# A grouped-convolution and mixed-experts chain: conv1 and the middle layer rebuilt from 32-row strips on row tiles, with the input rounded phase by phase

## The reference

```python
x = x + conv(x, W0)  + (cond @ cw0.T)[:, :, None] + bias      # 9 taps, 4 groups of 32 channels
x = x + (sum_k att1[b,k] * E1[k]) @ x + (att1 @ bias_k1)      # 8 experts, 128x128, 1x1 convolution
x = x + (sum_k att2[b,k] * E2[k]) @ x + (att2 @ bias_k2)
x = x + conv(x, W3)  + (cond @ cw3.T)[:, :, None] + bias      # as the first
```

## Time and profile before

| what | value |
|---|---|
| median of the runs | 2600.42 us |
| the profiled execution | 2600.42 us |
| its span, first to last instruction | 2598.5 us |
| TensorE busy | 2554.9 us, 98% |
| VectorE busy | 2277.4 us, 88% |
| ScalarE busy | 2077.8 us, 80% |
| queue with nearly all DMAs, share of 16 engines | 83.5% |
| mean granted TensorE clock | 0.995 of full |

### The profile page before, as it was taken

The page is one execution under the profiler, slowest core; times in us unless marked ns, Lnnn a source line. Parts: engine busy times, 40 slices in busy tenths (PEclk is TensorE's granted clock), DMA queues, the critical chain, the costliest instruction groups (busy, mean ns, idle before and its releaser), DMA issues.

```text
span 2598.5 us, 38320 instructions
## 1 busy us (share of the span) xinstructions
PE 2554.9 (98%) x11082; PEld 2071.6 (80%) x11082; DVE 2277.4 (88%) x3384; ACT 2077.8 (80%) x1940; POOL 3.7 (0%) x17
## 2 busy tenths in 40 slices
PE   6999999999999999999999999999999999999997
PEld 4788888888888888888888888888888888888885
DVE  7988888888888888888888888888888888888884
ACT  4788878888887888888788888878888887888885
POOL 0000000000000000000000000000000000000000
PEclk8999999999999999999999999999999999999998
DMA  5788888888888888888888888888888888888875
GB/s 193 284 317 317 320 318 314 321 324 316 317 320 318 313 321 324 316 316 320 318 314 321 324 316 316 321 318 313 321 323 317 317 320 317 315 320 322 317 300 210
DMA packets 335448, 808.75 MB, mean 311 GB/s; under 512 B 37066, under 2 KB 40146, under 8 KB 302674
## 3 DMA queue, kind: packets, MB, share of 16 engines
q1 hardware_dynamic: 333200, 807.16, 83.5%
q10 hardware_dynamic: 2242, 1.53, 0.2%
HBM read 137.45 MB, written 134.22 MB: 105 GB/s over the span
## 4 chain that ended last, share of the span: by engine, by line
PE 97%; DVE 2%; issue 0%; DMA 0%; ACT 0%; ACTq 0%; SPq 0%; DVEq 0%
PE pair L766 82%; PE quad L810 14%; PE pair L800 1%; DVE mixed L595 0%; PE quad L747 0%; DMA x_in<-in_x 0%; DVE w_hi L528 0%; DVE weighted L583 0%; DVE x_lo L504 0%; DVE x_lo L630 0%; DVE x_hi L627 0%; DMA x_ph<-x_ch 0%; DVE x_ch L569 0%; DVE w_lo L534 0%; DMA x_ch<-x_ph 0%
## 5 line engine op out<-in xcount | busy, mean ns | idle before, releaser
L766 PE MATMUL pair<-x_hi,w_hi 128*128 128x512 f32 x3072 | 1227.1, 399 | 8.7 <-DVE x_lo L643 5.4
L766 PE MATMUL pair<-x_hi,w_lo 128*128 128x512 f32 x3072 | 1213.1, 395 | 0.0
L766 PE MATMUL pair<-x_lo,w_hi 128*128 128x512 f32 x3072 | 1209.0, 394 | 0.0
L766 PEld LDWEIGHTS pair<-x_hi,w_lo 128*128 128x128 f32 x3072 | 579.6, 189 | 137.3
L766 PEld LDWEIGHTS pair<-x_hi,w_hi 128*128 128x128 f32 x3072 | 579.0, 188 | 136.4 <-DVE x_lo L643 5.8
L766 PEld LDWEIGHTS pair<-x_lo,w_hi 128*128 128x128 f32 x3072 | 581.6, 189 | 131.5
L595 DVE TENSOR_REDUCE mixed<-weighted 128x128 f32<-128x1152 f32 x256 | 576.9, 2254 | 0.1
L402 ACT COPY x_out<-x_ch 128x1024 f32<-128x1024 f32 x256 | 530.3, 2073 | 2.9 <-DMA x_ch<-x_ph 2.9
L351 ACT COPY x_ch<-x_in 128x1024 f32<-128x1024 f32 x256 | 531.0, 2076 | 1.9 <-DMA x_in<-in_x 1.9
L410 ACT COPY x_ph<-pair 128x512 f32<-128x512 f32 x512 | 314.8, 615 | 272.1 <-PE pair L766 272.1
L418 ACT ACTIVATE x_ph<-pair,bias_now 128x512 f32<-128x512 f32 x512 | 358.6, 700 | 216.2 <-PE pair L766 216.2
(11 more groups left out here) (80 smaller groups left out, 607.2 us busy)
## 6 DMA issues: line engine op xcount, KB each, us to landing
x_ph<-x_ch SPq DMA_DIRECT2D x1024, 256.0 KB, 2.6
x_ch<-x_ph SPq DMA_DIRECT2D x1024, 256.0 KB, 2.6
x_in<-in_x SPq DMA_DIRECT2D x128, 1024.0 KB, 5.5
out<-x_out SPq DMA_DIRECT2D x128, 1024.0 KB, 4.2
x_out<-in_W SPq DMA_DIRECT2D x8, 144.0 KB, 5.4
...
```

The source lines that it names most:

```text
L766: mm = nc.tensor.matmul(conv_bank[g % 2], w[l][:, m, g, :], x[:, g, m:m + N], start=(m == 0 and x is hi and w is w_hi), stop=(m == BLK - 1 ...
```

## The change

The program is rebuilt around one idea. Conv1 is computed in the **channel layout**: TensorE's 128 rows are used as four independent tiles of 32 rows, one for each group of 32 channels. For each of 12 strips (STRIPS = PH * BLK; strip d reads input phase d mod 4, shifted by d div 4) and each of the three parts, four matmuls of 32 rows by 512 columns are issued in a row, one per group, each into its own PSUM bank, each with its own 32x128 weights (`conv1_strips`). That is 144 matmuls where there were 36. Its output is in the phase layout, and the middle layer takes it as it is: 4 groups x 3 parts x 4 phases = 48 matmuls of 32 rows (`middle`), whose weights are rows of M laid out four times, once per phase (`m_rows`). Conv4 stays as it was, 36 matmuls of 128 rows. Two PSUM tiles of four banks, `banks[0]` and `banks[1]`, serve all layers: in step b conv1(b) and middle(b) use one, M(b+1) and conv4(b-1) the other.

What goes: the `cut` of x and the 4 DMAs of x to phase rows; the copy of x1 out of PSUM, its 4 DMAs back and its split from SBUF; the bias in the evacuation of x4. What comes:

- ScalarE rounds x straight from `x_in`, 2048 elements in one instruction that reads every fourth float (16 bytes apart) (`high_x`); VectorE's `low_x` reads `x_in` in the same way.
- ScalarE rounds x1 from PSUM in two halves (`high_x1`), VectorE subtracts from PSUM (`low_x1`).
- The bias of conv4 is added in `join`, which therefore waits for `bias4_ready`; VectorE's `set_bias4(b-2)` stands in its step b behind `split_x3(b-1)`.
- VectorE mixes the experts in 16 `scalar_tensor_tensor` instructions of 128x128 per batch in place of two products and two sums, and no longer carries the identity as a ninth expert.
- M is written to DRAM with one DMA (`save_m`) and read back with four (`spread_m`), from the same SyncE queue, a batch ahead.
- The order of ScalarE, VectorE, TensorE and SyncE is written anew.

The core of the diff, with lines of before marked - and of the changed kernel marked +:

```diff
-x_ch = sb("x_ch", [C, PH, N])
-x_ph = sb("x_ph", [C, G, N])
-x1_ph = sb("x1_ph", [C, G, N])
-x1_ch = sb("x1_ch", [C, PH, N])
+x_hi = sb("x_hi", [C, PH, N + 2 * HALO], f32r)
+w0_hi = sb("w0_hi", [C, STRIPS, PH, GROUP], f32r)
+m_saved = nc.dram_tensor("m_saved", [ODD, C, 2, C], f32).ap()
+m_rows = sb("m_rows", [C, ODD, G, 2, C], f32r)
+banks = [ctx.enter_context(nc.psum_tensor(f"banks{n}", [C, PH, N], f32)) for n in range(2)]
...
+    def save_m(b, slot):
+        sp.wait_ge(m_split, b + 1)
+        sp.dma_start(m_saved[slot, :, :, :], m_pair[:, :, :].bitcast(f32)).then_inc(m_stored, DMA)
+    def spread_m(b, slot):
+        sp.wait_ge(m_stored, DMA * (b + 1))
+        for q in range(PH):
+            sp.dma_start(m_rows[rows_of(q), slot, :, :, :].bitcast(f32),
+                         m_saved[slot, :, :, :].rearrange("(g c) t o -> c g t o", g=G)
+                         ).then_inc(m_spread, DMA)
...
+    def step(b, slot, first=False, load_next=True, last=False):
+        if not (first and slot == 0):
+            move_x3(b - 1)
+        if load_next:
+            load(b + 2, slot)
+        if not first:
+            store(b - 2, slot)
+        if not last:
+            save_m(b + 1, 1 - slot)
+        if not (first and slot == 0):
+            move_x4(b - 1, 0)
+        if not last:
+            spread_m(b + 1, 1 - slot)
+        if not (first and slot == 0):
+            move_x4(b - 1, 1)
...
-    def cut(b, slot, turn, half):
-        if half == 0:
-            act.wait_ge(x_loaded[slot], DMA * (turn + 1))
-            wait(act, x_moved, DMA * G * b)
-        phases = slice(half * PH // 2, (half + 1) * PH // 2)
-        nc.scalar.copy(x_ch[:, phases, :],
-                       x_in[:, slot, :].rearrange("c (n p) -> c p n", p=PH)[:, phases, :]
-                       ).then_inc(x_cut, 1)
-    def round_x(b):
-        act.wait_ge(x_moved, DMA * G * (b + 1))
-        wait(act, conv1_done, G * b)
-        nc.scalar.copy(x_hi[:, :, HALO:N + HALO], x_ph[:, :, :]).then_inc(x_hi_ready, 1)
+    def high_x(b, slot, turn):
+        act.wait_ge(x_loaded[slot], DMA * (turn + 1))
+        wait(act, conv1_done, G * b)
+        nc.scalar.copy(x_hi[:, :, HALO:N + HALO],
+                       x_in[:, slot, :].rearrange("c (n q) -> c q n", q=PH)
+                       ).then_inc(x_hi_ready, 1)
+    def high_x1(b, tile, half):
+        if half == 0:
+            wait(act, mid_done, PH * b)
+        act.wait_ge(conv1_done, G * b + (half + 1) * G // 2)
+        nc.scalar.copy(halves(x1_hi, half), halves(tile, half)).then_inc(x1_high, 1)
+    def join(b, slot, turn, half):
+        if half == 0:
+            act.wait_ge(x4_moved, DMA * G * (b + 1))
+            wait(act, x_stored[slot], DMA * turn)
+            act.wait_ge(bias4_ready, b + 1)
+        nc.scalar.activation(halves(x_out[:, slot, :].rearrange("c (n p) -> c p n", p=PH), half),
+                             halves(x4_ch, half), ACT.Identity, bias=bias4_now[:, :]
+                             ).then_inc(x_joined, 1)
+    def evacuate_x4(b, tile, half):
+        if half == 0:
+            wait(act, x4_moved, DMA * G * b)
+        act.wait_ge(conv4_done, G * b + (half + 1) * G // 2)
+        nc.scalar.copy(halves(x4_ph, half), halves(tile, half)).then_inc(x4_ready, 1)
+    def evacuate_x3(b, tile):
+        act.wait_ge(bias3_ready, b + 1)
+        act.wait_ge(mid_done, PH * (b + 1))
+        for half in range(2):
+            nc.scalar.activation(halves(x3_ch, half), halves(tile, half), ACT.Identity,
+                                 bias=bias3_now[:, :]).then_inc(x3_ready, 1)
+    def step(b, slot, turn, first=False, last=False):
+        if not first:
+            for half in range(2):
+                join(b - 2, slot, turn - 1, half)
+        for half in range(2):
+            high_x1(b, banks[slot], half)
+        if not last:
+            high_x(b + 1, 1 - slot, turn + slot)
+        if not (first and slot == 0):
+            for half in range(2):
+                evacuate_x4(b - 1, banks[1 - slot], half)
+        evacuate_x3(b, banks[slot])
...
+    def low_x(b, slot):
+        dve.wait_ge(x_hi_ready, b + 1)
+        nc.vector.tensor_tensor(x_lo[:, :, HALO:N + HALO],
+                                x_in[:, slot, :].rearrange("c (n q) -> c q n", q=PH),
+                                x_hi[:, :, HALO:N + HALO].bitcast(f32), ALU.subtract
+                                ).then_inc(x_lo_ready, 1)
+    def low_x1(b, tile, half):
+        dve.wait_ge(x1_high, 2 * b + half + 1)
+        nc.vector.tensor_tensor(halves(x1_lo, half), halves(tile, half),
+                                halves(x1_hi, half).bitcast(f32), ALU.subtract
+                                ).then_inc(x1_split, 1)
+    def mix_experts(b):
+        for k in range(K):
+            for l in range(2):
+                if k == 0:
+                    wait(dve, m_done, b)
+                else:
+                    dve.wait_ge(mix_ready[l], K * b + k)
+                nc.vector.scalar_tensor_tensor(mixed[l][:, :], expert[l][:, k, :],
+                                               mix[l][:, b, k:k + 1],
+                                               ident[:, :] if k == 0 else mixed[l][:, :],
+                                               ALU.mult, ALU.add).then_inc(mix_ready[l], 1)
+    def split_m(b, tile):
+        dve.wait_ge(m_done, b + 1)
+        nc.vector.tensor_copy(m_t[:, :].rearrange("p (c g) -> p c g", g=G),
+                              by_channel(tile[:, PH - 1, 0:C])).then_inc(m_ready, 1)
+        wait(dve, m_stored, DMA * b)
+        dve.wait_ge(m_ready, b + 1)
+        nc.vector.tensor_copy(m_pair[:, 0, :], m_t[:, :]).then_inc(m_high, 1)
+        dve.wait_ge(m_high, b + 1)
+        nc.vector.tensor_tensor(m_pair[:, 1, :], m_t[:, :], m_pair[:, 0, :].bitcast(f32),
+                                ALU.subtract).then_inc(m_split, 1)
...
+    def set_bias4(b):
+        wait(dve, x_joined, 2 * b)
+        nc.vector.tensor_scalar(bias4_now[:, :], bias4_ch[:, bass.ds(b, 1)], 0.0, None, ALU.add
+                                ).then_inc(bias4_ready, 1)
+    def step(b, slot, first=False, load_next=True, last=False):
+        if not (first and slot == 0):
+            split_x3(b - 1)
+        set_bias3(b)
+        if not first:
+            set_bias4(b - 2)
+        for half in range(2):
+            low_x1(b, banks[slot], half)
+        if not last:
+            split_m(b + 1, banks[1 - slot])
+            low_x(b + 1, 1 - slot)
+        if load_next:
+            mix_experts(b + 2)
...
+    def conv1_strips(b, tile, strips):
+        for d in strips:
+            shift, q = d // PH, d % PH
+            for w, x in ((w0_hi, x_hi), (w0_hi, x_lo), (w0_lo, x_hi)):
+                for g in range(G):
+                    mm = nc.tensor.matmul(
+                        tile[:, g, :], w[rows_of(g), d, :, :].rearrange("c q o -> c (q o)"),
+                        x[rows_of(g), q, shift:shift + N],
+                        start=(d == 0 and x is x_hi and w is w0_hi),
+                        stop=(d == STRIPS - 1 and w is w0_lo))
+                    if d == STRIPS - 1 and w is w0_lo:
+                        mm.then_inc(conv1_done, 1)
+    def conv1(b, tile):
+        pe.wait_ge(x_lo_ready, b + 1)
+        wait(pe, x4_ready, 2 * (b - 1))
+        conv1_strips(b, tile, range(STRIPS))
+    def middle_matrix(b, tile):
+        pe.wait_ge(mix_ready[0], K * (b + 1))
+        pe.wait_ge(mix_ready[1], K * (b + 1))
+        nc.tensor.matmul(tile[:, PH - 1, 0:C], mixed[0][:, :], mixed[1][:, :], start=True,
+                         stop=True).then_inc(m_done, 1)
+    def conv4(b, tile, m_aside):
+        for g in range(G):
+            pe.wait_ge(x3_split, G * b + g + 1)
+            if g == G - 1 and m_aside:
+                pe.wait_ge(m_ready, b + 3)
+            for m in range(BLK):
+                for w, x in ((w1_hi, x3_hi), (w1_hi, x3_lo), (w1_lo, x3_hi)):
+                    mm = nc.tensor.matmul(tile[:, g, :], w[:, m, g, :], x[:, g, m:m + N],
+                                          start=(m == 0 and x is x3_hi and w is w1_hi),
+                                          stop=(m == BLK - 1 and w is w1_lo))
+            mm.then_inc(conv4_done, 1)
+    def middle(b, slot, tile):
+        pe.wait_ge(m_spread, DMA * G * (b + 1))
+        pe.wait_ge(x1_split, 2 * b + 2)
+        for g in range(G):
+            for part, x in ((0, x1_hi), (0, x1_lo), (1, x1_hi)):
+                for q in range(PH):
+                    mm = nc.tensor.matmul(tile[:, q, :], m_rows[rows_of(q), slot, g, part, :],
+                                          x[rows_of(q), g, :],
+                                          start=(g == 0 and part == 0 and x is x1_hi),
+                                          stop=(g == G - 1 and part == 1))
+                    if g == G - 1 and part == 1:
+                        mm.then_inc(mid_done, 1)
+    def step(b, slot, last=False):
+        conv1(b, banks[slot])
+        if not last:
```

(73 more changed lines are left out.)

601 lines of the change are left out of this document (194 added, 407 removed).

## The result

The changed kernel takes **2962.55 us** (median of 4 runs, 2960.82 to 2963.98), the kernel before 2600.24 (2599.79 to 2600.62): ratio 1.1393, 95% interval 1.1373 to 1.1413, slower. Forecast were 2970 us and a range of 2780 to 3250. The profiled execution is the fastest of the four, 2960.82 us, with a span of 2959.0.

A forecast was written before the change was run, and what follows sets the result against it. A loop through all queues, closed by join waiting for bias4 behind the split, was taken to bound the kernel: eight terms sum to 22.7 us a step, T = 86.9 + 127 x 22.7 = 2970 us, range 2780 to 3250.

The forecast's parts named there:

- the ring: Loop from ScalarE's join through high_x1, high_x, x4 evacuation, SyncE, x3, split and bias4 to the next join: 22.7 us a step.
- TensorE still bounds: Rival: both loops are shorter than TensorE's 20.1 us a step, T = 2640 us; chance 0.04 for slower than before.
- first half of x4: ScalarE takes the first 1024 elements of x4 out of PSUM, without bias: 0.94 us.
- eight issues of SyncE: SyncE issues 2 moves of x4, 4 of M and 2 of x4 before x3: 5.0 us.
- first x3 issue to first cast: From SyncE's first issued move of x3 to the first cast of its split: 2.38 us.
- The landing: Arrival of x3's moved data, from SyncE's first issue to the first cast: 2.38 us, measured with queues nearly idle.
- the second loop: Loop through TensorE (conv4's last group, middle layer), x3 and join, bypassing high_x and SyncE's eight issues: 22.0 us.
- q: Time of one set of four 32-row matmuls on TensorE: taken as 0.2326 us, bounded by 0.213 and 0.93.
- The 0.32 for two changes: TensorE switches between whole array and row tiles twice a step, 0.16 us of pipeline each time.
- 86.9: Microseconds for start, end and what lies outside the span, taken as unchanged, give or take 15 us.
- 4.05 + 3.2 = 7.3: VectorE's low_x plus 16 mixing products, us, hidden within the 8.3 us between high_x and x3's first landed group.
- the case with low_x and the mixing not hidden: VectorE's low_x and mixing take 4.05 + 5.6 = 9.7 us, adding 1.3 to the step: P = 24.1.

## Why the prediction was right

**The mechanism.** "So every step waits for the step before": the one edge that closes the ring, VectorE's bias behind the split, was taken away alone, and 313 of the 362 us came back. The rival "TensorE still bounds" gives the time of that kernel: forecast 2640, measured 2649.77.

**The period.** 22.7 was forecast and 22.58 measured, 22.5 from the sixth on. Its terms, from the rows above and the timeline around them:

| term of the sum | forecast | measured |
|---|---|---|
| first half of x4 | 0.94 | 0.9 |
| eight issues of SyncE | 5.0 | 4.53, and 0.50 for the jump back in every other step |
| first x3 issue to first cast | 2.38 | 2.5 in the steps that go through the queue; 1021.56 - 1018.52 = 3.0 in those through TensorE |
| split of x3 | 4.26 | 4.2 |
| biases | 0.28 | 0.3 |
| join | 4.0 | 3.80 |
| high_x1 | 2.0 | 1.86 |
| high_x | 3.83 | 3.79 |

The queue's 5.0 came out by luck: an issue of M takes 0.49 us (1.97 for four) and not 0.62, and the jump of SyncE's loop, which I had not looked for, filled the rest. The landing was taken from a nearly idle queue and is 0.1 longer in this loop, 0.6 in the steps of the other; the join and high_x1 are 0.34 shorter. In a step that goes through the queue the measured terms add up to 22.4. That the time came out within 0.3% is in part luck: errors of both signs cancel, and the second loop, taken as shorter, sets the other half of the steps.

**The second loop.** "So even a faster queue or a cheaper high_x leaves some 22.0": both were run, and both leave 22.1 (2906.84 and 2906.73 us). That it ties with the first, so that the two alternate, was not foreseen; I had it as the shorter one. The forecast took the x3 evacuations as done while the queue was still issuing, and expected x3's moves later than x3 was ready. They are later by 0.3 us in every other step only; in the rest the queue waits for x3.

**TensorE.** q = 0.2326 was taken and 0.23 measured, and TensorE's own step is 20.08 us against the 20.1 of the sum. The loads of the four tiles don't queue: 48 sets with 192 loads stand as close as 48 matmuls did. The 0.32 for two changes between row tiles and whole ones is visible, 0.37 from the last set to M and 0.32 from conv4's first matmul to its second, where 0.23 is usual, and again at the middle layer. Matmuls on one and the same row tile also follow each other 0.23 us apart (the run with the tiles in turn), so four tiles side by side give 4.0 times here. TensorE: Matmul & The Clock Gate in the Trainium skill (Part 3, Measured speedup vs the span model) has 3.07 for them, which was estimated to give 23.5 us a step of TensorE; this kernel shows 20.08.

**Start and end.** Outside the 127 periods lie 63.8 us ahead of x3's first move, 2959.0 - 2930.83 = 28.2 behind its last and 1.8 outside the span, 93.8 in the profiled execution, where 86.9 was taken; the 15 us of the range held it. It makes up for half of what the shorter period takes off: 7 us more against 127 x 0.12 = 15 less.

**VectorE.** Here the sum was right by little. The forecast hid `low_x` and the mixing, "4.05 + 3.2 = 7.3", with the lower bound of 3.2 us for 16 products. They take 3.8 + 4.3 = 8.1 us, and the room taken was 8.3. In the step shown VectorE was ready 0.68 us before the data of x3. I looked at this only as a term that might be added, and not as a loop of its own, which it is: it stood at 21.8 under the other two and became the bound as soon as they were opened.

**Two sums of the forecast are off.** At q = 0.35 TensorE's work is 8.91 + 48 x 0.35 = 25.7 us and T = 3350, so that 3250 is reached at q = 0.333 already; and the case with low_x and the mixing not hidden gives P = 24.0, not 24.1. Neither enters the 2970.

**Where the gain went.** The change freed 2277.4 - 1965.9 = 311 us of VectorE and 2077.8 - 1734.6 = 343 of ScalarE, and the DMA share in mid-program fell from 0.86 to 0.59. None of these bounded the kernel before. It paid with one dependence between engines, at the end of a list.
